# Quantised cross attention tile by tile with its neighbours' projections beside it, and the exponential's bias made on VectorE

## The reference

```python
x = x + _L1_attn_ref(_layernorm(x, axis=-1), ...)     # causal, 16 heads of 16, keys and values by a low-rank path
x = x + _L1_xattn_ref(_layernorm(x, axis=-1), ctx_2048, ...)
x = x + _L1_ffn_ref(_layernorm(x, axis=-1), ...)      # 64 routes, 32 of them experts, 8 for each token
...
q = _fq_sym(q, axis=-1)          # 8-bit rounding per token and head
k = _fq_sym(k, axis=-1)
v = _fq_sym(v, axis=2)
attn = jnp.einsum('bhqd,bhkd->bhqk', q, k)
attn = jax.nn.softmax(attn.astype(jnp.float32), axis=-1)
attn = _fq_unsigned(attn, axis=-1)     # rounding to 255 steps of the row's maximum
out = jnp.einsum('bhqk,bhkd->bhqd', attn, v)
return out @ Wp + bp
```

## Time and profile before

| what | us |
|---|---|
| median of three runs | 686.37 |
| lowest, highest | 685.69, 686.54 |
| the profiled execution's own time | 689.58 |
| its span on the core | 687.5 |

### The profile page before, as it was taken

The page is one execution under the profiler, slowest core; times in us unless marked ns, Lnnn a source line. Parts: engine busy times, 40 slices in busy tenths (PEclk is TensorE's granted clock), DMA queues, the critical chain, the costliest instruction groups (busy, mean ns, idle before and its releaser), DMA issues.

```text
span 687.5 us, 10676 instructions
## 1 busy us (share of the span) xinstructions
PE 468.5 (68%) x3820; PEld 299.1 (44%) x3820; DVE 451.6 (66%) x778; ACT 318.3 (46%) x550; POOL 249.7 (36%) x380
## 2 busy tenths in 40 slices
PE   3956816567887997867787888877858137556540
PEld 2525703353555775655343333433337126434330
DVE  5897999968495767477888897988835861101003
ACT  1343305534203442457888888898842103333320
POOL 5443479972800000430111111111101045888870
PEclk9987867968998999898555555566557557999995
DMA  8630000000000000001999999999995165895546
GB/s 309 182 131 1 0 0 1 1 0 0 2 1 2 2 2 2 1 1 35 184 177 178 180 179 186 174 183 184 186 176 190 40 203 142 218 199 110 90 68 193
DMA packets 170259, 70.73 MB, mean 103 GB/s; under 512 B 142240, under 2 KB 167776, under 8 KB 170208
## 3 DMA queue, kind: packets, MB, share of 16 engines
q1 hardware_dynamic: 164064, 61.15, 41.8%
q0 software_dynamic: 6144, 8.92, 7.5%
HBM read 27.56 MB, written 8.93 MB: 53 GB/s over the span
## 4 chain that ended last, share of the span: by engine, by line
PE 28%; DVE 23%; issue 17%; ACT 12%; DMA 11%; POOL 8%; POOLq 0%; SPq 0%; DVEq 0%; ACTq 0%
ACT KV L610 8%; PE ps L662 5%; DMA KV<-KV 5%; DVE AT L1167 4%; POOL b L484 3%; DMA A<-x_rows,slot_token 3%; PE ps L816 3%; POOL sums L505 2%; PE ps L848 2%; ACT A L594 2%; DMA sums<-A,slot_token 2%; POOL A L491 2%; PE ps L831 2%; PE ps L654 2%; PE ps L829 1%
## 5 line engine op out<-in xcount | busy, mean ns | idle before, releaser
L1237 DVE TENSOR_REDUCE nm<-ps 128x1 f32<-128x1024 f32 x128 | 154.3, 1223 | 27.3 <-PE ps L894 25.6
L610 ACT ACTIVATE KV<-ps,b,sq 128x1024 int16<-128x1024 f32 x128 | 153.3, 1201 | 29.2 <-POOL b L484 14.7
L894 PE MATMUL ps<-A 128*128 128x512 bf16 x256 | 125.0, 590 | 34.7 <-ACT KV L610 32.8
L484 POOL TENSOR_SCALAR b<-nm,sq 128x1 f32<-128x1 f32 x128 | 33.8, 264 | 174.4 <-DVE nm L1237 148.9
L903 PEld LDWEIGHTS ps<-VI,KV 128*128 128x128 f16 x1024 | 55.0, 113 | 74.3 <-issue 53.4
L1326 DVE TENSOR_TENSOR AT<-AT,ps 128x128 f32<-128x128 f32 x32 | 9.2, 288 | 86.7 <-ACT AT L632 86.7
L505 POOL DMA_INDIRECT sums<-A,slot_token x32 | 50.8, 1586 | 21.5 <-ACT A L639 12.1
L903 PE MATMUL ps<-VI,KV 128*128 128x16 f16 x1024 | 50.9, 179 | 7.7 <-DMA KV<-KV 7.6
L413 POOL TENSOR_SCALAR veps<-mv 128x4 f32<-128x4 f32 x12 | 3.0, 248 | 142.6 <-DVE mv L981 142.5
L491 POOL DMA_INDIRECT A<-x_rows,slot_token x32 | 34.8, 1089 | 37.7 <-issue 35.9
L517 ACT ACTIVATE XT<-ps 128x256 f32<-128x256 f32 x48 | 18.3, 386 | 55.8 <-PE ps L654 55.7
(11 more groups left out here) (271 smaller groups left out, 1001.4 us busy)
## 6 DMA issues: line engine op xcount, KB each, us to landing
A<-in SPq DMA_DIRECT2D x32, 256.0 KB, 3.6
A<-in SPq DMA_DIRECT2D x32, 128.0 KB, 4.0
A<-in SPq DMA_DIRECT2D x2, 1024.0 KB, 14.2
sums<-zeros SPq DMA_DIRECT2D x4, 512.0 KB, 5.3
KV<-KV SPq DMA_TRANSPOSE x128, 3.3
A<-sums SPq DMA_DIRECT2D x8, 256.0 KB, 4.7
X<-in SPq DMA_DIRECT2D x1, 1024.0 KB, 6.0
ctxT<-in SPq DMA_DIRECT2D x1, 1024.0 KB, 8.6
```

What stands on the lines that cost most here:

```text
L484: g.tensor_scalar(b5[:, n % 4:n % 4 + 1], nm5[:, n % 4:n % 4 + 1], sq5[:, q, h:h + 1], LN255, ALU.mult, ALU.add).then_inc(S["bias5_ready"], 1)
L610: a.activation(Y5[:, n % 4, :], ps[:, 2 * (n % 3):2 * (n % 3) + 2, :], ACT.Exp, scale=sq5[:, q, h:h + 1], bias=b5[:, n % 4:n % 4 + 1], acc ...
L894: done = T.matmul(ps[:, 2 * (n % 3) + c, :], QT5[:, h, q * P:(q + 1) * P], KT5[:, h, c * 512:(c + 1) * 512], start=True, stop=True)
L1237: v.tensor_reduce(nm5[:, n % 4:n % 4 + 1], ps[:, 2 * (n % 3):2 * (n % 3) + 2, :].rearrange("p a c -> p (a c)"), AX.X, ALU.max, negate=True ...
```

## The change

**The causal attention.** The mask matmuls go. POOL instead clears the upper triangle behind the exponential, with one `affine_select` of 128x512 for each of the 32 exponentials. The matmuls with `onesf` go as well: column 16 of each head's 32 value columns is one, so that the sum comes out beside the values. DVE transposes the result in 32x32 blocks, takes the reciprocal of 128x8, multiplies 128x8x16 and transposes back. The output projection, the normalisation and the query projection are done here for tiles 0 and 1 alone.

**Between the attentions.** The keys and the queries are transposed by DMA (one for each tile), in 64 rows a head instead of 128, so that two heads share the partitions. `KT5` lies where the context and the weights of layer 0 were, and its DMAs are issued as soon as these are free.

**The quantised attention** now has tiles outside and heads inside. DVE makes the bias itself, behind the maximum. `Y5` and `PT5` have six buffers. Beside each tile run, at fixed units, the pieces of its neighbours: for the tile before it the transpose ("at"), the `wp5` projection ("wp"), the transpose of the normalised rows ("x5") and the logits ("lg"); for the tile two ahead the output projection of the causal attention ("wo"), a transpose ("x4") and the `wq5` projection ("q5"). A piece of PE waits until the result of the piece before it was read.

**The experts.** Only two of the four lists stand ahead of the experts, the others go in at experts 0 and 8. Four experts' weights are loaded ahead instead of eight.

```diff
+YB, LAG5 = 6, 6
+LIST_AT = [0, 0, 0, 8]
...
-        QT5 = A[:, 0:8192].bitcast(BF16).rearrange("p (h c) -> p h c", h=H)
-        KT5 = A[:, 8192:16384].bitcast(BF16).rearrange("p (h c) -> p h c", h=H)
+        XTs = A[:, 15872:16384].rearrange("p (s k c) -> p s k c", s=2, k=KD)
+        QT5 = ctx_sb[:, 0:6, :].rearrange("p t c -> p (t c)").bitcast(BF16).rearrange("p (s h c) -> p s h c", s=3, h=H // 2)
+        Y5 = A[:, 4096:4096 + 512 * YB].bitcast(I16).rearrange("p (b c) -> p b c", b=YB)
+        PT5h = A[:, 8192:8192 + 512 * YB].bitcast(F16).rearrange("p (b k c) -> p b k c", b=YB, k=8)
...
+        AT_H, WP_H, WO_H, X5_H, X4_H, LG_H, Q5_H = 1, 3, 5, 7, 9, 10, 12
+        SIDE5 = []
+        for q in range(NT + 1):
+            SIDE5 += [("at", q - 1), ("wp", q - 1)] * (q >= 1) + [("wo", q + 2)] * (q + 2 < NT) + [("x5", q - 1)] * (q >= 1)
+            SIDE5 += [("x4", q + 2)] * (q + 2 < NT) + [("lg", q - 1)] * (q >= 1) + [("q5", q + 2)] * (q + 2 < NT)
...
-                sp.dma_start(WG[:, e % WS, :, :], wgu_in[e, :, :].rearrange("(k p) c -> p k c", p=P)).then_inc(wg_loaded[e % 8], 16)
-                sp.dma_start(WD[:, e % WS, :], wdown_in[e, :, :]).then_inc(wg_loaded[e % 8], 16)
...
+            sp.wait_ge(S["out3_psum"], NT)
+            sp.wait_ge(S["zeros_ready"], 2)
+            for t in range(NT):
+                sp.wait_ge(S["kq_step"], 8 * (t + 1))
+                sp.dma_start_transpose(KT5[:, :, t * P:(t + 1) * P], kpart_rows[:, t, :]).then_inc(S["k5T_loaded"], 16)
+
+            def query_T(t):
+
+                sp.wait_ge(S["q5i_ready"], t + 1)
+                if t >= 3:
+                    sp.wait_ge(S["s5_psum"], H * (t - 2))
+                sp.dma_start_transpose(QT5[:, t % 3, :, :], kpart_rows[:, t, :]).then_inc(S["q5T_loaded"], 16)
...
+            query_T(0)
+            query_T(1)
             for n in range(U5):
                 sp.wait_ge(S["exp5_ready"], n + 1)
-                if n >= 4:
...
+                    sp.wait_ge(S["p5V_done"], n - YB + 1)
+                sp.dma_start_transpose(PT5[:, n % YB, :, :], Y5[:, n % YB, :]).then_inc(p5T_loaded[n % YB], 16)
+                q = at_unit(n, X5_H + 1)
+                if q is not None and q >= 1:
+                    store_rows(q - 1)
+                q = at_unit(n, Q5_H + 3)
+                if q is not None and q + 2 < NT:
...
+            for e in range(4):
                 load_weights(e)
...
-            g.memset(A[:, 0:8192], 0.0).then_inc(S["pad5_ready"], 1)
-            for n in range(U5):
-                h, q = n // NT, n % NT
-                pool.wait_ge(S["max5_ready"], n + 1)
-                if n >= 4:
-                    pool.wait_ge(S["exp5_ready"], n - 3)
-                g.tensor_scalar(b5[:, n % 4:n % 4 + 1], nm5[:, n % 4:n % 4 + 1], sq5[:, q, h:h + 1], LN255, ALU.mult, ALU.add).then_inc(S["bias5_ready"], 1)
...
+            for n in range(2 * G4):
+                pool.wait_ge(S["exp4_ready"], n + 1)
+                e = E4[n // 2 % 3][:, 2 * (n % 2):2 * (n % 2) + 2, 0:2 * P].rearrange("p j (a c) -> p j a c", a=2)
+                g.affine_select(out=e, in_=e, compare_op=ALU.is_ge, fill=0.0, base=0,
...
+                    ln_rstd("r", q - 1, q)
+                    if q < NT:
+                        ln_apply("r", q - 1)
...
+                    t = q + 2
+                    ln_rstd("q", t, t + 1)
+                    ln_apply("q", t)
+                    add_bp(t)
...
-                        T.matmul(ps[:, banks[r], 0:SEQ], identb[:, :], causalT[:, :].unsqueeze(1).to_broadcast([P, 2, P]), start=True, stop=True)
...
-                    for lo, w in ((0, [V4[:, 2 * b:2 * b + 2, 4 * g + r, :] for r in range(4)]), (SEQ, [onesf[:, 0:64].rearrange("p (t c) -> p t c", t=2)] * 4)):
-                        for r in range(4):
-                            T.matmul(ps[32 * r:32 * r + 32, bank, lo:lo + SEQ], w[r][:, 0, :], e[:, r, P:P + SEQ], start=True, stop=False)
-                        for r in range(4):
-                            last = T.matmul(ps[32 * r:32 * r + 32, bank, lo + P:lo + SEQ], w[r][:, 1, :], e[:, r, 0:P], start=False, stop=True)
...
+                    for r in range(4):
+                        T.matmul(ps[32 * r:32 * r + 32, bank, 0:SEQ], V4[:, 2 * b, 4 * g + r, :], e[:, r, P:P + SEQ], start=True, stop=False)
+                    for r in range(4):
+                        last = T.matmul(ps[32 * r:32 * r + 32, bank, P:SEQ], V4[:, 2 * b + 1, 4 * g + r, :], e[:, r, 0:P], start=False, stop=True)
...
+                    rows = slice(64 * (h % 2), 64 * (h % 2) + 64)
...
+                        done = T.matmul(ps[:, 2 * (n % 3) + c, :], QT5[rows, q % 3, h // 2, :], KT5[rows, h // 2, c * 512:(c + 1) * 512], start=True, stop=True)
...
+                if at_unit(n, AT_H) is not None and q >= 1:
+                    wait_side_read(pe, side - 1)
+                    pe.wait_ge(S["o5_ready"], q)
+                    side_T(AT[:, q - 1, :], bank, 0, "at5T_psum")
+                    side += 1
+                if at_unit(n, WP_H) is not None and q >= 1:
+                    wait_side_read(pe, side - 1)
+                    pe.wait_ge(S["vscale_ready"], 6)
+                    side_project(0, wp5, D, bank, D, "wp_psum")
+                    side += 1
...
+                for n in range(2, NE // EG):
+                    if s == LIST_AT[n] + 3:
+                        list_grid(n)
+                    if s == LIST_AT[n] + 6:
+                        list_spread(n)
...
-                v.reciprocal(r4[:, u % 2, :], ps[:, bank, SEQ:2 * SEQ]).then_inc(S["r4_ready"], 1)
...
+                v.transpose(oq.rearrange("p n c -> p (n c)"), ps[:, bank, 0:SEQ]).then_inc(S["oq4_ready"], 1)
+                dve.wait_ge(S["oq4_ready"], u + 1)
+                v.reciprocal(r, oq[:, :, HD]).then_inc(S["r4_ready"], 1)
...
+                v.tensor_tensor(on[:, :, 0:HD], oq[:, :, 0:HD], r.unsqueeze(2).to_broadcast([P, 8, HD]), ALU.mult).then_inc(S["om4_ready"], 1)
+                dve.wait_ge(S["om4_ready"], u + 1)
+                v.transpose(QT4[:, g, b * SEQ:(b + 1) * SEQ], on.rearrange("p n c -> p (n c)")).then_inc(S["on4_ready"], 1)
...
+            for n in range(U5 + LAG5 + H):
+                if n < U5:
+                    h, q = n % H, n // H
+                    dve.wait_ge(S["s5_psum"], n + 1)
+                    v.tensor_reduce(nm5[:, n % 4:n % 4 + 1], ps[:, 2 * (n % 3):2 * (n % 3) + 2, :].rearrange("p a c -> p (a c)"), AX.X, ALU.max, negate=True).then_inc(S["max5_ready"], 1)
+                    dve.wait_ge(S["max5_ready"], n + 1)
+                    if n >= 4:
+                        dve.wait_ge(S["exp5_ready"], n - 3)
+                    v.tensor_scalar(b5[:, n % 4:n % 4 + 1], nm5[:, n % 4:n % 4 + 1], sq5[:, q, h:h + 1], LN255, ALU.mult, ALU.add).then_inc(S["bias5_ready"], 1)
+                q = (n - LAG5) // H
+                bank = 6 + (q + 1) % 2
+                if at_unit(n, 0) is not None and q >= 1:
+                    dve.wait_ge(S["p5V_done"], q * H)
+                    v.reciprocal(r5[:, :], sum5[:, (q - 1) * H:q * H]).then_inc(S["r5_ready"], 1)
+                    dve.wait_ge(S["r5_ready"], q)
+                    v.tensor_tensor(AT[:, q - 1, :].rearrange("p (h d) -> p h d", d=HD), ps[:, bank, 0:D].rearrange("p (h d) -> p h d", d=HD),
+                                    r5[:, :].unsqueeze(2).to_broadcast([P, H, HD]), ALU.mult).then_inc(S["o5_ready"], 1)
+                if at_unit(n, WP_H) is not None and q >= 1:
+                    dve.wait_ge(S["xbias_ready"], q)
+                    side_residual(q - 1, bank, D, "wp_psum", "xp_ready")
+                    side_stats("r", q - 1, "xp_ready", q)
+                if at_unit(n, WO_H) is not None and q + 2 < NT:
+                    side_residual(q + 2, bank, 0, "wo_psum", "xo_ready")
+                    side_stats("q", q + 2, "xo_ready", q + 3)
+                if at_unit(n, WP_H + 2) is not None and q == NT:
+                    side_norm("r", q - 1)
+                if at_unit(n, LG_H) is not None and q >= 1:
+                    dve.wait_ge(S["lg_psum"], q)
+                    v.tensor_copy(L6[:, q - 1, :], ps[:, bank, D:D + NROUTE]).then_inc(S["lg_ready"], 1)
```

More of the change, by code:

```diff
@@ L923, in _ @@
+                if at_unit(n, Q5_H) is not None and q + 2 < NT:
+                    wait_side_read(pe, side - 1)
+                    pe.wait_ge(S["x4T_ready"], q + 3)
+                    side_project(1, wq5, D, bank, 0, "q5_psum")
+                    side += 1
             pe.wait_ge(S["router_ready"], 1)
@@ L928, in _, with list_grid @@
             last.then_inc(S["pos6_psum"], 1)
-            pe.wait_ge(S["const6_ready"], 4)
-            for n in range(NE // EG):
+            def list_grid(n):
                 pe.wait_ge(S["onehot_ready"], 2 * (n + 1))
```

505 lines of the change are left out of this document (277 added, 228 removed).

## The result

The changed kernel took **663.35 us** at the median (660.63 to 667.43, 4 runs) against 686.45 us for the kernel before in the same measurement (685.69 to 694.46, 4 runs): a ratio of **0.964, 95% interval 0.956 to 0.973**. It is faster, and by 23 us, not the 55 that were predicted: the median lies outside the range of 611 to 655. The profiled execution took 660.63 us for a span of 658.7. Here and in the experiments the ratios leave out slow executions, those more than 1.5% above the fastest of their kernel, while the medians and ranges take in all.

What follows compares the result with a forecast made beforehand. PE was taken to bound the causal pass, and a ring of three bank pairs through several engines the quantised attention. Terms -65.5 + 34 - 15 - 8.5 = -55 us took the median from 686.4 to 631 us, range 611 to 655.

Steps and rivals of the forecast that it cites:

- VectorE becomes the bound, 1.40 us a unit: Quantised attention: with the bias on DVE, 128 units at 1.40 us make 179 us, and its other work adds in full.
- Units and its own work for the tiles: Quantised attention: 179 us of units, 13 us for tiles behind, 17.5 us for tiles ahead.
- 0.4 of waiting for the output projection: Quantised attention, tile ahead: DVE waits 0.4 us for PE's longest piece, four matmuls of 0.42 us at the low clock.
- Most pieces fit ... 3 us: Quantised attention: most PE pieces hide beside DVE's work; a transpose and the logits cost 0.3 to 0.5 us, 3 us together.
- POOL beside DVE, 9 us: Quantised attention: 37 POOL instructions hold up DVE's biases by a quarter microsecond each, 9 us; 48 by the skill's rule.
- The causal pass and what lay behind it: Causal pass and the stretch up to the quantised attention: its start moves from 318.6 to 253 us, -65.5 us.
- Behind it, -15: Stretch after the quantised attention: seven of eight tiles are already done beside the units, leaving 15 us; -15 us, ends -12 and -18.
- the lists, -8.5: Before the experts: two lists took 9.6 us, the third now stands on DVE before expert 1; -8.5 us, not given back later.
- the pipeline was not broken: Rival, chance 0.05: 46 PE pieces each empty the ring of bank pairs, about 1.3 us, growing the quantised stage by 60.
- The sign that was named for it: Quantised attention: DVE idle for more than a tenth of the stage with PE's scores ending it would prove the prediction wrong.
- POOL is dearer: Rival, chance 0.17: a 1.42 us select in the causal pass gives 646 us; biases held 0.8 us each as well, 666.
- The pieces are cheaper: Rival, chance 0.15: no contention, select 0.6, PE at high clock; -7 us causal pass, -15 quantised attention, 609 us.

Runs made afterwards that it cites:

- quarter of the output projection: Changed kernel with three of the four matmuls of every output projection in the quantised stage left out; 651.02 us, ratio 0.949.
- projections ahead: Changed kernel with output projections moved out of the quantised loop, tiles 2 to 5 into the causal pass, 6 and 7 behind the first quantised scores; 659.89 us.
- all pieces cut down: Changed kernel, quantised loop keeping one of four output projection matmuls and one of two for the projection, queries and logits; 637.88 us, ratio 0.928.
- two groups in one block: Changed kernel with two head groups sharing one 32-column block, so a tile's output projection is two matmuls instead of four; 654.66 us, ratio 0.951.
- half of the value product: Changed kernel with four of the eight matmuls of the quantised attention's value product, half of the keys left out; 658.61 us, ratio 0.963.
- pieces split in two: Kernel with two groups in one block, each projection inside the loop split over two neighbouring units; 659.70 us, ratio 0.964 against the kernel before.

## Why the prediction was wrong in size

**The account that holds.** In every variant of the changed kernel with the bias on VectorE the quantised stage is VectorE's busy time, plus its waits for PE, plus 7 to 9 us. A stage is always an engine's busy and idle time; what the table shows is that the busy time hardly moves and that the idle time that does is all ended by PE:

| kernel | DVE busy | DVE's waits for PE | sum | stage |
|---|---|---|---|---|
| changed | 202.4 | 28.8 | 231.2 | 239.8 |
| quarter of the output projection | 202.3 | 16.7 | 219.0 | 226.8 |
| projections ahead | 200.0 | 16.2 | 216.2 | 224.6 |
| all pieces cut down | 200.8 | 5.1 | 205.9 | 214.0 |
| two groups in one block | 202.9 | 21.1 | 224.0 | 231.7 |
| half of the value product | 202.2 | 23.3 | 225.5 | 233.5 |
| pieces split in two | 203.8 | 24.0 | 227.8 | 234.9 |

The 7 to 9 us are, in the changed kernel, 7.3 us of gaps of under 0.15 us each between VectorE's 352 instructions and 1.1 us from its last one to the end of the last exponential.

A piece starts as DVE starts a maximum, so 1.4 us of it are free; the rest is a wait, and then comes DVE's own work for that tile. For the output projection that gives 3.76 - 1.4 + 1.05 = 3.4 us above a plain unit; the trace has 3.3 at the median of the tiles, 1.6 with two matmuls (2.05 us: 1.7 by the rule) and 1.0 with one (1.2 us: 1.05). The projection of the tile behind (2.05 us, the same own work) has 1.8. The rule also fits both half-misses: slack in plain units doesn't help, since DVE sets their pace; and of a split piece each half stands ahead of scores, where the waits are then found (23.2 us in 47 places). That second reading is argued from the waits and not shown by a run of its own.

**Point by point.**
- *VectorE becomes the bound, 1.40 us a unit*: right for a plain unit, 1.38. It was busy for 84% of the stage, and not for over 90% as its signs had it. *Units and its own work for the tiles*: 207 us in the sum (179 + 13 + 17.5 less the 2.4 of waiting), 202.4 measured.
- *"0.4 of waiting for the output projection ... (four matmuls of 6.71 / 16 = 0.42 at the low clock)"*: **the step that failed.** The price of a matmul was taken per record, half of what it is (0.94 us at that clock), so the piece was put at 1.7 us and is 3.76; the wait is 2.1 us a tile, 12.8 in all instead of 2.4.
- *"Most pieces fit ... 3 us"*: failed with it. The other pieces and the scores cost 16.0 us of waiting (7.2 + 5.0 + 3.8). The same slip put a piece at "0.5 to 1.8" us, when they are 1.2 to 3.8, and even by those numbers scores and value product (1.25) and a piece of 1.8 do not fit beside 1.4 plus side work that itself has to wait for the piece.
- *POOL beside DVE, 9 us*: none in the bias. The 128 biases took 0.212 to 0.216 us, the 31 that ran beside an elementwise instruction of GpSimd too. (In the earlier trace rows the wait is 1.29 less 0.34, and not the 1.29 that the 48 us were worked out from.) That was luck, and it kept the error from being larger: +23.4 of waits, +7 of gaps and ends, where 1.5 had been put, -9 and -5 make the 17 us.
- *The causal pass and what lay behind it*: right, -64.0 against -65.5. About 2 us of the gain are the clock, which was 1.00 all through this pass; with a granted clock of 0.77 in its first 15 us the same code took 45.6 us and not 43.6. The rows below show groups 1.92 us apart (predicted 1.95) and a select of 0.7 us (0.9), hidden:

```profile
217.26 0.71 PE L919 MATMUL ps<-A 32*128 32x256 f32 x8 [0.98 <-ACT A L670]
...
218.22 1.51 ACT L670 ACTIVATE A<-ps 128x768 f32<-128x768 f32 x2 [0.40 <-PE ps L921]
...
219.10 1.34 POOL L536 TENSOR_SCALAR_AFFINE_SELECT A<-A 128x512 f32<-128x512 f32 x2 [0.57 <-ACT A L670]
...
219.18 0.71 PE L919 MATMUL ps<-A 32*128 32x256 f32 x8 [0.98 <-ACT A L670]
```

- *Behind it, -15, and the lists, -8.5*: right in kind, 13.2 and 5 to 6.4. With two lists ahead, the second is made while GpSimd gathers the first rows, so taking lists away spares less than their own time.
- *+4.4 us ahead of the second causal pass* goes with the clock and not with the edits. The granted clock was 0.85 there against 0.95 before (windows 176:215.3 and 176:210.9). Two variants have the same instructions as the changed kernel up to that pass: the one with half of the value product reached it at 208.2 with a granted clock of 0.88 between 176 and 190 us, the one with four buffers at 218.0 with 0.52; the changed kernel had 0.59. With the 0.88 that the kernel before had too, the changed code is thus 2.7 us sooner there, and not later (between 150 and 176 us it had 0.93 then, against 0.84, so that isn't the edits alone either). The first of them started its quantised attention at 253.8, where 253 was predicted. So spans and starts of single profiles differ by up to 10 us through this stretch alone, and variants are better compared stage by stage. Why the clock differs there stays open.
- *The rivals*: the pipeline was not broken, but that rival came nearest. It asked what a piece costs and set the turning point at 1.2 us for each of 46; the waits of 28.8 us are 0.6 each. The sign that was named for it showed in part: PE ended 12% of the stage as idle time of DVE, more than the tenth that was named, but its scores ended only 3%; the rest stood ahead of the residuals and of the query projections' results. *POOL is dearer* fell: its two prices were 1.42 us for the select (0.7 measured) and 0.8 us for a held bias (none). *The pieces are cheaper* argued with a stage that asks less of PE; it asked more, 219.6 us busy of 239.8, and the clock stayed at 0.54.

**What stays open.** Whether the changed kernel with all of its projections at the full clock would reach the predicted 223 us could not be tried, and no run shows why the clock of this stage stays low.

## What to carry to other kernels

Before a piece of work is put into a loop as hidden, write down when it starts against the engine that bounds the loop: what is free is the time until that engine asks for its result, here 1.4 us, once for each piece, and slack elsewhere added next to nothing to it. Price it from a row that counts matmuls in the source and not records in the trace, at the clock of the stage that it moves to. When a piece is on the path anyway, make it smaller (two head groups in one block won 9 us) before moving or splitting it, which won nothing here. And before comparing two profiles by their spans, compare the granted clock of the stretches that the edit leaves alone.

## What the runs showed of the hardware

- A 128x256 matmul of 32-bit data cost 0.94 us at a granted clock of 0.50 and 0.465 us at 1.00 (3.76 us for four, 3.72 for eight).
- The granted clock of the quantised stage lay near the lower of its two levels, 1.2 GHz (0.50 to 0.59 in all variants) though PE was busy for up to 94% of it. It went up for a moment behind an output projection, then down again. The windows before, in, behind and after it:

```profile
299.00:306.10 7.10, 7.10 (x45) 2.68 (x44) 5.74 (x11) 4.44 (x9) 0.88 (x3) 0.50 1.12 172
306.10:309.80 3.70, 3.70 (x16) 2.55 (x12) 1.55 (x3) 2.59 (x4) 1.17 (x1) 0.50 0.81 156
309.80:313.70 3.90, 3.13 (x33) 1.27 (x32) 3.61 (x7) 1.26 (x3) 2.29 (x4) 0.92 0.45 84
313.70:325.00 11.30, 11.21 (x71) 4.85 (x72) 9.55 (x18) 8.13 (x15) 1.27 (x3) 0.51 0.99 153
```

- VectorE beside GpSimd: of the 15 recorded products of two SBUF operands (128x128) in the second causal pass four took 0.60 to 0.73 us instead of 0.29. Each of the four began 0.05 to 0.2 us into a select of 128x512 and ended some 0.14 us behind it. The other eleven took 0.29 us, eight of them with a select beside them for a part of their time. The biases of 128x1 lost nothing. The Trainium skill, GPSIMD Engine Reference, section 1, has contention for VectorE instructions with two SBUF inputs or in a 2-port mode; the trace agrees with it on the product.

```profile
221.01 1.34 POOL L536 TENSOR_SCALAR_AFFINE_SELECT XT<-XT 128x512 f32<-128x512 f32 x2 [0.57 <-ACT XT L670]
...
221.76 0.73 DVE L1323 TENSOR_TENSOR A<-XT,r 128x128 f32<-128x128 f32 x1
```
